# Layer 1 experts: the second product of three blocks in four in half-precision parts, and a lag of four blocks

## The reference, cut to what matters

```
x      = ln2_out.reshape(-1, H)                     # 4096 tokens, H = 128
gate   = softmax(einsum('th,eh->te', x, router_weight))
top_probs, top_idx = top_k(gate, 2)
h_mid  = gelu(einsum('th,ehf->etf', x, moe_w1))     # 8 experts, F = 256
expert_out = einsum('etf,efh->eth', h_mid, moe_w2)
moe_out    = einsum('eth,et->th', expert_out, weights)
return hidden_after_attn + moe_out
```

## Time and profile before

| | us |
|---|---|
| time of three runs, median (lowest, highest) | 866.43 (864.79, 869.19) |
| span of the profiled execution | 862.7 |
| median less span (the execution's own time outside the span is not given) | 3.7 |
| lowest run less span | 2.1 |
| experts' part: first up product to the end of the span | 648.88 to 862.7 |

### The profile page before, as it was taken

How to read it: one execution, slowest core, us unless ns; L and a number is a source line. 1 busy time by engine, 2 the same in 40 slices (tenths; PEclk the granted TensorE clock), 3 DMA queues, 4 the chain that set the end, 5 groups by cost and what they waited for, 6 DMA issues and landing times. The chain is left out here.

```text
span 862.7 us, 26300 instructions
## 1 busy us (share of the span) xinstructions
PE 727.4 (84%) x10112; PEld 545.5 (63%) x10112; DVE 639.6 (74%) x1802; ACT 408.4 (47%) x777; POOL 198.2 (23%) x317
## 2 busy tenths in 40 slices
PE   3468898888888889889999477887759999999997
PEld 2245565555556777667787245665547888888886
DVE  7568877787868989888996577887665766666653
ACT  3123223322235656656655365665635555554553
POOL 3333222232534212330200553342011110011100
PEclk9569989998898999999999599999998999999999
DMA  4000000140034221122200000000000000000000
GB/s 103 9 22 13 23 21 21 33 88 18 24 99 100 82 78 50 53 66 79 81 15 14 4 2 5 5 4 4 5 3 2 13 13 0 12 12 12 12 13 13
DMA packets 33082, 26.43 MB, mean 31 GB/s; under 512 B 9740, under 2 KB 29912, under 8 KB 32984
## 3 DMA queue, kind: packets, MB, share of 16 engines
q1 hardware_dynamic: 29944, 24.07, 10.5%
q10 hardware_dynamic: 3040, 0.98, 0.5%
HBM read 13.51 MB, written 7.34 MB: 24 GB/s over the span
## 5 line engine op out<-in xcount | busy, mean ns | idle before, releaser
L1931 PEld LDWEIGHTS bank<-w2r,hme 128*128 128x128 f32 x1024 | 132.2, 191 | 15.6 <-ACT hme L1876 1.4
L1931 PE MATMUL bank<-w2r,hme 128*128 128x128 f32 x1024 | 135.5, 276 | 0.0
L1876 ACT ACTIVATE hme<-bank,b 128x512 f32<-128x512 f32 x128 | 86.5, 687 | 96.3 <-PE bank L97 96.3
L984 ACT ACTIVATE P<-bank 128x512 f32<-128x512 f32 x128 | 76.6, 598 | 76.2 <-PE bank L1130 75.0
L1900 DVE SCALAR_TENSOR_TENSOR Xq<-bank,wgte,Xq 128x128 f32 (+1 forms) x256 | 72.1, 344 | 51.1 <-PE bank L1931 38.3
L1056 DVE TENSOR_SCALAR bank<-bank 128x512 f32<-128x512 f32 x128 | 89.6, 700 | 15.2 <-PE bank L1121 14.4
L1064 DVE TENSOR_REDUCE mx<-bank 128x4 f32<-128x512 f32 x128 | 87.1, 681 | 1.4 <-PE bank L1104 1.3
L500 ACT ACTIVATE w2r<-bank 128x512 f32<-128x512 f32 x40 | 23.9, 597 | 114.5 <-PE bank L814 82.8
L1130 PE MATMUL bank<-mT,negsel 128*128 128x128 f16 x512 | 51.0, 223 | 13.9 <-DVE bank L1056 12.6
L95 PE MATMUL bank<-xTe,w 128*128 (+1 forms) x128 | 48.8, 381 | 5.5 <-PEq L1295 5.5
L825 PE MATMUL bank<-w_raw,hm 128*128 128x128 f32 x320 | 50.3, 308 | 2.9 <-DVE X L739 2.8
(11 more groups left out here) (382 smaller groups left out, 1785.3 us busy)
## 6 DMA issues: line engine op xcount, KB each, us to landing
cross_q<-qh SPq DMA_DIRECT2D x24, 128.0 KB
Q<-cross_q SPq DMA_DIRECT2D x8, 384.0 KB, 3.9
X<-in_x SPq DMA_DIRECT2D x8, 256.0 KB, 2.8
Xq<-X SPq DMA_DIRECT2D x32, 64.0 KB
cross_k<-kh SPq DMA_DIRECT2D x16, 128.0 KB
Yq<-Y SPq DMA_DIRECT2D x32, 64.0 KB
out_x<-Xq SPq DMA_DIRECT2D x32, 64.0 KB, 1.7
cload<-in_ctx SPq DMA_DIRECT2D x8, 192.0 KB, 2.5
```

Of the source, the lines that this page charges most:

```text
L984: act.activation(P[j][:], TB[u % 3][:], ACT.Exp, scale=SCALE).then_inc(s["p_ready"], 1)
L1876: act.activation(hm[:, p % HR], UP[p % RING][:], ACT.Gelu_apprx_tanh, bias=b1[:, p:p + 1]).then_inc(s["gelu"], 1)
L1931: last = pe.matmul(Y[f % 2][:, cols], hm[:, p % HR, cols], w2r[:, p], start=(p % 2 == 0 and i == 0), stop=(p % 2 == 1), skip_group_check=True)
```

## The change

Of every four blocks the first three (`HALVED`: p % 4 != 3, 12 of a group's 16, 96 of 128 in all) make the down product in f16 parts: ACT, after the gelu and a wait for its own result, copies `hm` to `hp[0]` (f16, high part); POOL subtracts, `hp[1] = hm - hp[0]` (f16, low part); PE makes 12 f16 products instead of four f32 ones. The weights `w2r` are split once by DVE, at the start of this part, in four pieces. The block with p % 4 == 3 stays as it was. The down product follows its up product by LAG = 4 blocks instead of two, and the combine at slot p handles block p - 5 instead of p - 3.

```diff
-    NB, LAG, RING, HR = 2 * NE, 2, 4, EXPERT_RING
+    NB, LAG, RING, HR = 2 * NE, 4, 4, EXPERT_RING
+    HALVED = [p for p in range(NB) if p % 4 != 3]
...
+    w2p = [room.sb(f"w2_{i}", [128, NB, C], F16) for i in range(2)]
+    hp = [room.sb(f"hp{i}", [128, HR, N], F16) for i in range(2)]
+    q = room.sems("w2_high w2_low hm_high hm_low")
...
+                    if cur(g) and p in HALVED:
+                        pool.wait_ge(q["hm_high"], place(g, p) + 1)
+                        after(pool, s["down_psum"], NB * g + p - HR + 1)
+                        pool.tensor_tensor(hp[1][:, p % HR], hm[:, p % HR], hp[0][:, p % HR], ALU.subtract
+                                           ).then_inc(q["hm_low"], 1)
                     if nxt(g) and p == 1:
                         expert_root(pool, e, g + 1)
...
+                        if p in HALVED:
+                            act.wait_ge(s["gelu"], k + 1)
+                            act.activation(hp[0][:, p % HR], hm[:, p % HR], ACT.Copy).then_inc(q["hm_high"], 1)
...
+            dve.wait_ge(keep["w2_in"], 16)
+            for i in range(4):
+                at = slice(4 * i, 4 * i + 4)
+                dve.tensor_copy(w2p[0][:, at], w2r[:, at]).then_inc(q["w2_high"], 1)
+                dve.wait_ge(q["w2_high"], i + 1)
+                dve.tensor_tensor(w2p[1][:, at], w2r[:, at], w2p[0][:, at], ALU.subtract).then_inc(q["w2_low"], 1)
             over_rest(dve, step, G - 1)
-            for f in (NE - 2, NE - 1):
+            for f in (NE - 3, NE - 2, NE - 1):
                 combine((G - 1, 2 * f + 1))
...
-                pe.wait_ge(s["gelu"], NB * g + p + 1)
+                if p in HALVED:
+                    if not isinstance(g, int) or g == 0:
+                        pe.wait_ge(q["w2_low"], p // 4 + 1)
+                    pe.wait_ge(q["hm_low"], place(g, p) + 1)
+                else:
+                    pe.wait_ge(s["gelu"], NB * g + p + 1)
...
-                    last = pe.matmul(Y[f % 2][:, cols], hm[:, p % HR, cols], w2r[:, p], start=(p % 2 == 0 and i == 0),
-                                     stop=(p % 2 == 1), skip_group_check=True)
+                    begin, end = p % 2 == 0 and i == 0, p % 2 == 1
+                    if p in HALVED:
+                        last = split_product(pe, Y[f % 2][:, cols], [h[:, p % HR, cols] for h in hp], [w[:, p] for w in w2p],
+                                             start=begin, stop=end, skip_group_check=True)
+                    else:
+                        last = pe.matmul(Y[f % 2][:, cols], hm[:, p % HR, cols], w2r[:, p], start=begin, stop=end,
+                                         skip_group_check=True)
                 last.then_inc(s["down_psum"], 1)
```

More of the change, by code:

```diff
@@ L1844, in late, with place @@
         return (h, (p - lag) % NB) if cur(h) else None
-    with nc.Block() as block:
+    ctx = ExitStack()
+    room = Room(nc, ctx, "parts")
+    w2p = [room.sb(f"w2_{i}", [128, NB, C], F16) for i in range(2)]
+    hp = [room.sb(f"hp{i}", [128, HR, N], F16) for i in range(2)]
+    q = room.sems("w2_high w2_low hm_high hm_low")
+    def place(k, p):
+        return len(HALVED) * k + HALVED.index(p)
+    with ctx, nc.Block() as block:
         @block.sync
```

## The result

| | before | changed |
|---|---|---|
| median (lowest, highest) of 20 runs each, us | 865.15 (862.54, 869.19) | 869.0 (865.3, 872.61) |
| ratio, 95% interval | | 1.004 (1.0028 to 1.0053) |
| span of the profiled execution, us | 862.7 | 868.0 |
| experts' part, first up product to the end | 213.8 | 868.0 - 650.44 = 217.6 |

The changed kernel is slower by 0.4%, 3.9 us by the medians; the sign was forecast, at less than half the size (+8.9 by the sum). That is less than the 0.5% (4.3 us) which the prediction had counted as a difference, and 869.0 lies not in the forecast's own range (871 to 882) but in that of the rival "in between" (862 to 871). The profiled execution lost 3.7 us in the experts' part and began that part 1.6 us later (650.44 instead of 648.88), at work that the change doesn't touch.

The account below looks back on a forecast made before the run. PE's own work bounds the experts' part. Loop groups fall from 26.16 to 23.5 us, plus 3.8 waits: 27.3; six +6.8, group 0 +1.9, group 7 +0.1 make +8.9, span 871.6, plus 3.7: 875 us (8-in-10 range 857 to 889).

Parts of the forecast that it names:

- in between: Rival: each stall half as long, a loop group near 26.1 us, time 862 to 871, no difference; chance 0.18.
- the walk without exclusion: Same loop group walked with no DVE/POOL exclusion: waits 1.4 us, 24.9 us a group, time 856.
- it is POOL's tensor_tensor that shuts DVE out: POOL's tensor_tensor, of which the change adds 96, blocks DVE's port instructions; four of xn's form beside tensor_scalar took 1.10 us.
- Sum 3.8, so a loop group takes 27.3.: Loop group: PE's waits sum to 3.8 us on top of 23.5, 1.1 more than 26.16; six groups +6.8.
- down 12: Block 12's down product: PE waits 0.8 us for slot 14's combine, as block 12's subtraction holds the last compare 1.0.
- down 14: Block 14's down product: PE waits 1.0 us for slot 0's combine, after an is_lt wait and DVE's loop-turn idle.
- down 0: Block 0's down product: PE waits 0.6 us for slot 2's combine, done at 9.1 and wanted at 8.5.
- turn: The turn (L1741): PE waits 0.8 us for xn, done by 12.4 between subtractions and wanted at 11.75.
- down 2: Block 2's down product: PE waits 0.6 us for slot 4's combine behind xn, done 13.5 and wanted 13.0.
- PE's waits need not cost clock: PE's added waits need not lower its clock: with PE busy 80 of 100 us the granted clock was 1.00.
- The port costs little: Rival: DVE's small instructions fall into gaps, xn and compare waits together under 1 us, time 856; chance 0.24.
- POOL becomes the bound: Rival: a subtraction takes 1.6 us, POOL needs 21.8 of 23.5, a group takes 30.2, time 893; chance 0.16.

Follow-up runs that it names:

- one-input instruction: Changed kernel with GpSimd's two-input subtraction replaced by a multiplication by 1 of one input over all 512 columns: 851.34 us, ratio 0.9841 to the kernel before.
- zero fill: Changed kernel with GpSimd subtracting 16 of 512 columns, the low parts filled with zeros at GpSimd's start: 854.9 us, ratio 0.9872 to the kernel before.
- filled hole: Changed kernel with 19 unused 128x512 products in TensorE's row of group 0 ahead of the turn: 866.96 us, ratio 1.003 to the kernel before.
- group 0 mended: Changed kernel with group 0's first twelve blocks left in f32 and the weights split in slots 4, 5, 7 and 8: 863.12 us, ratio 0.9973.
- eight blocks in the right places: Changed kernel with only blocks 0, 1 and 5 to 10 halved, group 0 in f32: 855.69 us, ratio 0.9897 to the kernel before.
- eight in the wrong ones: Changed kernel with every second block halved (0, 2, ... 14), group 0's first twelve in f32: 870.2 us, ratio 1.0054 to the kernel before.
- twelve spread evenly: Changed kernel's halved blocks (p % 4 != 3) kept in the loop groups, group 0's first twelve in f32: 863.12 us, ratio 0.9973 to the kernel before.

## Why the prediction was right in sign and wrong in size

**Right.** The f16 down product takes 0.67 (702.89 to 703.56 in the changed kernel). ScalarE's copy is 0.63 (0.62 estimated), and the exponential's result arrives on VectorE 1.55 after its table load began, as before. The exclusion is real, and costs at the compare L1816 and at xn; where both are nearly free of it a group is 24.83 (24.9 by the walk without exclusion; the small holds that are left there make the agreement partly luck). TensorE waits for `Xq` ahead of the down products of blocks 12, 14, 0 and 2. Group 7 is unchanged within 0.1.

The page "SBUF — State Buffer" of the Trainium skill, Who interferes with whom, has the exclusion held for the whole of an instruction. The traces agree in that xn and the subtractions strictly take turns (4.50 and 4.49 for four each in group 0); they differ in that VectorE gets in some 0.2 before the reported end. What the prediction had wrong is "it is POOL's tensor_tensor that shuts DVE out": GpSimd's one-input instruction held L1820 to 0.63 instead of 0.19, and its zero fill held a cast to 3.75 instead of 0.42.

**The step that failed: "Sum 3.8, so a loop group takes 27.3."** It is the term of the loop group's waits, right in kind and too large: 26.33 - 23.5 = 2.8 was measured. Place by place (measured: the start in the timeline less the one that the pace of the products ahead gives, as 707.02 instead of 706.41 for down 12; together they are the 2.8):

| wait ahead of | predicted | measured |
|---|---|---|
| down 12 | 0.8 | 0.6 |
| down 14 | 1.0 | 0.7 |
| down 0 | 0.6 | 0.7 |
| turn | 0.8 | 0.2 |
| down 2 | 0.6 | 0.5 to 0.65 |

The turn is more than half of the miss. xn ended 11.7 into the group instead of 12.4, for two reasons that the rows show. A subtraction takes 1.16, not the 1.27 taken from the sum's two f32 inputs, and xn meets two of them; and every stop of VectorE before came 0.2 to 0.4 earlier than in the walk. That is a small error of timing, but a wait is the difference of two times that lie close together, and the loop groups repeat it: 1.0 in each of groups 2 to 6 is 4.9 us. What share the shorter subtraction has was not tried by itself.

**A second miss, of the opposite sign: group 0.** I had 27.5 and it took 29.17. That xn ends near 13.4 was right (12.99 to 13.05), although the split took 5.2 instead of 4.5, its last cast held to 1.38 by the first subtraction; the 14 from the turn on became 16.1. "PE's waits need not cost clock" failed here: it was read from a stretch with many short holes, and behind one hole of 4.48 us the granted clock was 0.51. The trace of the kernel before had shown the same, at the start of this very part: TensorE stood idle for 5.51 us, and from 649 to 651 the granted clock was 0.50, with the first up product at 0.58 instead of 0.38:

```profile
648.88 0.58 PE L95 MATMUL bank<-xTe,w 128*128 128x512 f16 x1 [5.51 <-PEq L1295]
```

The filled hole shows the clock's share, 2.2. The short holes of the loop groups did not cost clock (1.00 in 700 to 730). The page "TensorE: Matmul & The Clock Gate" of the Trainium skill, Part 1, has the throttled state as the default, which activity releases; the trace agrees (0.51 behind the hole, 1.00 from 668 on).

**Not forecast: group 1 at 25.49.** Its first turn comes 10.9 after its start, 0.9 sooner than in the loop groups. It is not that VectorE catches up while TensorE runs slowly in group 0: in the kernel with the filled hole, at a clock of 1.00, group 1 takes 25.49 too (673.63 to 699.12). The timeline of group 0 shows another order:

```profile
677.98 0.42 DVE L1816 TENSOR_TENSOR c8e<-c8e 128x256 f32<-128x256 f32 x1
...
681.02 1.03 DVE L1821 COPY wgte<-sele 128x32 f32<-128x32 f32 x1
```
```profile
678.32 3.68 POOL L1876 TENSOR_TENSOR hp<-hme,hp 128x512 f16<-128x512 f32 x3 [2.90 <-ACT hp L1896]
```

Here the compare comes before the subtraction and is free; L1819 and L1821 behind it are held in its place (0.83 and 1.03), and VectorE's two idles of 0.51 behind L1807 and L1816 are absent. So the combine of slot 0 starts 3.22 into group 1 instead of 4.10, and the first waits are shorter; no run tried this by itself. Groups 0 and 1 together came to +2.9, near the +3.0 forecast for both, but by luck: the first was forecast 1.7 too short, the second 1.8 too long.

**A term beside the kernel.** The forecast added 3.7 to the span, the distance of the median before from one profiled execution. After the change that distance is 869.0 - 868.0 = 1.0. So 2.7 of the 6 us between 875 and 869.0 come from this term and not from the walk.

**The rivals.** "The port costs little" is refuted for this order of blocks: L1816, two of xn and L1801 are held for 3 us a group together. What it promised was reached once the subtractions were moved away from them. "POOL becomes the bound" is refuted by 1.16 a subtraction and GpSimd busy for 17.3 of 30 us. What came is nearest to the rival "in between": a group near 26.1 was 26.33.

## What to carry to other kernels

When two engines exclude each other, their busy shares say little; lay the two timelines side by side and see which instruction of the one that others wait for meets which of the other. Then place the optional work (here, which blocks are halved) in the stretches where the excluded engine has slack: with group 0 mended, eight blocks in the right places gave 1.0%, eight in the wrong ones cost 0.5%, and twelve spread evenly gave 0.3%. A start 0.05 us to one side or the other decides which instruction is held, so that a walk can place such a wait only roughly. And look at one-off groups by themselves: group 0, with its subtractions beside xn and the idle stretch that came of them, cost more here (3.6 us) than the six loop groups did together (0.1).

## What the runs showed of the hardware

- One idle stretch of 4.48 us of TensorE was followed by about 4 us at a granted clock of 0.51, in which a 128x512 f16 product is reported at 0.63 instead of 0.38 us. With the stretch filled by unused products the clock stayed at 1.00. Behind idle stretches of 2.63 and 2.65 us, in two kernels, it was 0.57 and 1.00.
- GpSimd's 128x512 instructions to f16: 1.16 us with two inputs (f32 and f16), 0.63 with one (f32), 0.22 for two inputs of 16 columns. The first two were both seen to hold VectorE, the one-input form too (L1820 0.63 instead of 0.19), and so was a zero fill with no input (a cast of 0.42 took 3.75 beside 3.51 us of it). Where VectorE's compare had begun first, GpSimd's instruction took 0.78 instead of 0.62.
- Instructions as small as a copy of 32 columns (0.18) can be held for 0.9 more by GpSimd's subtraction (L1821).
